# Making the expert layer's normalised tokens and gate scores inside the self-attention loop

## The reference

```python
x = x + _L0_attn_ref(_layernorm(x), L0_attn_W_qkv)     # 16 heads of 32, sequences of 64 tokens
x = x + _L0_ffn_ref(_layernorm(x), L0_ffn_w_gate, L0_ffn_c_fc, L0_ffn_c_proj)

# in _L0_ffn_ref, xf = the normalised tokens, 1024 x 512, w_gate 512 x 8
scores = jax.nn.softmax(xf @ w_gate, axis=-1)
weights, idx = jax.lax.top_k(scores, 2)
# every token goes to its two experts (silu(a) * g, then c_proj); the outputs are weighted and added
```

## Time and the profile before

| what | value |
|---|---|
| median of 3 runs | 2301.62 us (2297.68 to 2303.34) |
| the profiled execution | 2300.68 us, its span 2298.8 us |
| mean granted TensorE clock | 0.934 of full speed |
| TensorE busy, whole span | 2048.7 us (89%) |
| self-attention, first q transpose of tile 0 to that of tile 7 | 178.44 to 311.36 us |
| self-attention, tile 7 until its last product is read | 311.36 to 330.83 us |
| from there to the first routing instruction (L774) | 330.83 to 366.00 us |
| routing, owners and slots | 366.00 to 378.46 us |
| the four weight arrays of L710 | issued 334.40 to 335.82 us, the last landed 18.8 us after its issue |
| scatter, until TensorE's first expert instruction | 378.46 to 406.42 us |

### The profile page before, as it was taken

How to read it: one execution, slowest core, us unless ns; L and a number is a source line. 1 busy time by engine, 2 the same in 40 slices (tenths; PEclk the granted TensorE clock), 3 DMA queues, 4 the chain that set the end, 5 groups by cost and what they waited for, 6 DMA issues and landing times. The chain is left out here.

```text
span 2298.8 us, 29289 instructions
## 1 busy us (share of the span) xinstructions
PE 2048.7 (89%) x9908; PEld 1410.4 (61%) x9908; DVE 1119.8 (49%) x2292; ACT 902.9 (39%) x1668; POOL 122.3 (5%) x137
## 2 busy tenths in 40 slices
PE   7978973899999958999999999999969999867998
PEld 4647762555555547787878777777746666523443
DVE  4655652001101136354453536364448888739992
ACT  5743320111111134444444435354436666525550
POOL 0000003000000011000000000000000000002320
PEclk9989975999999989999999999999988999668999
DMA  7310014787777522010100000012040000010000
GB/s 264 123 51 1 0 65 192 282 315 310 284 314 315 219 69 92 15 46 33 40 32 27 32 27 32 27 46 87 1 162 1 1 1 1 1 78 0 1 14 23
DMA packets 32725, 208.18 MB, mean 91 GB/s; under 512 B 4243, under 2 KB 4244, under 8 KB 25110
## 3 DMA queue, kind: packets, MB, share of 16 engines
q1 hardware_dynamic: 30102, 199.02, 23.0%
q0 software_dynamic: 2560, 8.39, 1.1%
HBM read 186.95 MB, written 20.45 MB: 90 GB/s over the span
## 5 line engine op out<-in xcount | busy, mean ns | idle before, releaser
L108 PE MATMUL PS<-cT,qs 128*128 128x512 f32 x1152 | 295.2, 402 | 9.0 <-ACT pb L1242 7.0
L108 PE MATMUL PS<-pT,cN 128*128 128x512 f32 x1152 | 270.1, 393 | 1.7 <-DVE pT L1337 1.7
L108 PEld LDWEIGHTS PS<-cT,qs 128*128 128x128 f32 x1152 | 209.2, 189 | 59.5 <-issue 15.0
L900 PE MATMUL PS<-W,xgT 128*128 128x384 f32 x736 | 242.8, 489 | 1.4 <-ACT xgT L923 1.4
L108 PEld LDWEIGHTS PS<-pT,cN 128*128 128x128 f32 x1152 | 214.0, 188 | 45.2 <-DVE pT L1337 1.9
L900 PEld LDWEIGHTS PS<-W,xgT 128*128 128x128 f32 x736 | 140.7, 191 | 104.0 <-issue 11.4
L108 PE MATMUL PS<-ws,xT 128*128 128x512 f32 x672 | 183.3, 429 | 6.4 <-DVE ws L571 4.9
L108 PEld LDWEIGHTS PS<-ws,xT 128*128 128x128 f32 x672 | 133.8, 201 | 52.8 <-issue 21.9
L1332 DVE TENSOR_REDUCE nmax<-PS 128x1 f32<-128x512 f32 x128 | 87.7, 685 | 157.0 <-PE PS L108 156.4
L951 DVE TENSOR_TENSOR hid<-gated,PS 128x384 f32<-128x384 f32 x46 | 23.4, 551 | 277.6 <-PE PS L876 235.6
L884 PE MATMUL PS<-W,hT 128*128 128x512 f32 x276 | 124.5, 601 | 10.4 <-ACT hT L917 10.4
(11 more groups left out here) (226 smaller groups left out, 3198.7 us busy)
## 6 DMA issues: line engine op xcount, KB each, us to landing
W<-in_fc SPq DMA_DIRECT2D x23, 3072.0 KB, 12.5
W<-in_proj SPq DMA_DIRECT2D x23, 1536.0 KB, 6.5
cT<-in_ctxT SPq DMA_DIRECT2D x16, 768.0 KB, 5.3
ct_in<-in_ctxT SPq DMA_DIRECT2D x16, 768.0 KB
cn_in<-in_ctxN SPq DMA_DIRECT2D x16, 768.0 KB
W<-in_w SPq DMA_DIRECT2D x2, 4096.0 KB, 12.9
routed_x<-zero SPq DMA_DIRECT2D x23, 256.0 KB, 5.4
xg<-routed_x SPq DMA_DIRECT2D x23, 256.0 KB, 5.7
```

Of the source, the lines that this page charges most:

```text
L108: mm = nc.tensor.matmul(out, lhs(m, s), rhs(n, s), start=(opens and (s, m, n) == terms[0]), stop=((s, m, n) == terms[-1]))
L900: mm = nc.tensor.matmul(ps[c][:, 0:HFE], xgT[:, k, :], fc[u][:, k, c * HFE:(c + 1) * HFE], start=(k == 0), stop=(k == DK - 1))
```

## The change

The normalisation, the GpSimd copy, the transposes and the gate products of the expert layer are issued inside the self-attention's pass. After `x` of tile i is final, VectorE makes its statistics and, behind the copy of v, the normalised tile `gxn`; GpSimd makes the power and copies the tile to `xn`. TensorE transposes tile i-1 behind the projections (`gate_turn`, bank 7), and multiplies it by the gate weights between the first and the second group of probability transposes (`gate_scores`, in a free piece of bank 6); ScalarE copies the transposed tile (`gate_xT`) and the 8 scores per token (`gate_out`) to `logit`. Tile 0 is written out ahead of the loop, since it has no predecessor; tile 7's transposes and products follow at the end. `gate` is loaded at the start of the self-attention. The expert layer's loop over the tiles goes, and its first reduction reads the scores from SBUF. The diff, cut:

```diff
@@ -445,18 +445,43 @@
+        xn, logit = e.xn, e.logit
+        gate, gxT = sbuf("gate3", [P, DK, NE]), sbuf("xT3", [P, DK, P])
+        gxn = sbuf("xn3", [P, D])
+        gst, gmv, gve, grs = sbuf("st3", [P, 6]), sbuf("mv3", [P, 2]), sbuf("ve3", [P, 1]), sbuf("rs3", [P, 1])
+        s_gate, g_var, g_rstd, g_norm = sem("s_gate3"), sem("var3"), sem("rstd3"), sem("norm3")
+        g_turned, g_xT, g_mm, g_sb = sem("turned3"), sem("xT3_sb"), sem("g_mm3"), sem("g_sb3")
+        g_kept, g_seen = sem("kept3"), sem("seen3")
...
+            @block.sync
+            def _(sp):
+                sp.dma_start(gate[:, :, :], a["gate"]).then_inc(s_gate, 16)
...
+                def gate_rstd(i):
+                    pool.wait_ge(g_var, BASE + i + 1)
+                    nc.gpsimd.tensor_tensor(grs[:, :], gve[:, :], cn[:, CN_MHALF:CN_MHALF + 1],
+                                            ALU.pow).then_inc(g_rstd, 1)
+
+                def gate_keep(i):
+                    pool.wait_ge(g_norm, BASE + i + 1)
+                    nc.gpsimd.tensor_copy(xn[:, bass.ds(i, 1), :].rearrange("p o d -> p (o d)"),
+                                          gxn[:, :]).then_inc(g_kept, 1)
...
                     ln.pool(pool, i + 2)
+                    gate_rstd(i)
+                    gate_keep(i)
+                gate_rstd(NT - 1)
+                gate_keep(NT - 1)
...
+                def gate_turn(i):
+
+                    pe.wait_ge(g_norm, BASE + i + 1)
+                    for kk in range(DK):
+                        tr = nc.tensor.transpose(ps[7][:, kk * P:(kk + 1) * P],
+                                                 gxn[:, kk * P:(kk + 1) * P], ident)
+                    tr.then_inc(g_turned, 1)
+
+                def gate_scores(i):
+
+                    pe.wait_ge(g_xT, BASE + i + 1)
+                    for kk in range(DK):
+                        mm = nc.tensor.matmul(ps[6][:, DK * S:DK * S + NE], gxT[:, kk, :], gate[:, kk, :],
+                                              start=(kk == 0), stop=(kk == DK - 1))
+                    mm.then_inc(g_mm, 1)
+
+                pe.wait_ge(s_gate, BASE + 16)
                 ln.tensor(pe, 0)
                 project(0)
 
-                def tile(i, last):
+                def tile(i, first, last):
...
                         project(i + 1)
+                    if not first:
+                        gate_turn(i - 1)
                     pe.wait_ge(e_sb, BASE + 2 * i + 2)
                     for g in TURN:
+                        if not first and g == TURN[1]:
+                            gate_scores(i - 1)
+                        if not first and g == TURN[3]:
+                            pe.wait_ge(g_sb, BASE + i)
...
-                with pe.Fori(0, NT - 1) as i:
-                    tile(i, False)
-                tile(NT - 1, True)
+                tile(0, True, False)
+                with pe.Fori(0, NT - 2) as i:
+                    tile(i + 1, False, False)
+                tile(NT - 1, False, True)
+                pe.wait_ge(o_read, BASE + NT)
+                gate_turn(NT - 1)
+                gate_scores(NT - 1)
...
+                def gate_xT(i):
+                    act.wait_ge(g_turned, BASE + i + 1)
+                    nc.scalar.activation(gxT[:, :, :].rearrange("p k t -> p (k t)"), ps[7],
+                                         ACT.Copy).then_inc(g_xT, 1)
+
+                def gate_out(i):
+                    act.wait_ge(g_mm, BASE + i + 1)
+                    nc.scalar.activation(logit[:, bass.ds(i, 1), :].rearrange("p o e -> p (o e)"),
+                                         ps[6][:, DK * S:DK * S + NE], ACT.Copy).then_inc(g_sb, 1)
...
                     if not last:
                         take(i + 1)
+                    if not first:
+                        gate_xT(i - 1)
                     for g in range(2):
                         act.wait_ge(pt_mm, BASE + 4 * i + TURN.index(g) + 1)
                         act.wait_ge(o_mm, BASE + i)
                         nc.scalar.activation(pT[:, g * DK:(g + 1) * DK, :].rearrange("p m t -> p (m t)"),
                                              ps[3 + g], ACT.Copy).then_inc(pt_act, 1)
-
-                with act.Fori(0, NT - 1) as i:
-                    tile(i, False)
-                tile(NT - 1, True)
+                        if g == 0 and not first:
+                            gate_out(i - 1)
...
+                gate_xT(NT - 1)
+                gate_out(NT - 1)
...
-                    nc.vector.tensor_tensor(x[:, i, :], x[:, i, :], o[:, :], ALU.add)
+                    ch.link(nc.vector.tensor_tensor(x[:, i, :], x[:, i, :], o[:, :], ALU.add))
+                    row = bass.ds(i, 1)
+                    ve.sem_inc(g_seen)
+                    ch.link(nc.vector.bn_stats(gst[:, :], x[:, row, :].rearrange("p o d -> p (o d)")))
+                    ve.sem_inc(g_seen)
+                    ch.link(nc.vector.bn_aggr(gmv[:, :], gst[:, :]))
+                    nc.vector.tensor_scalar(gve[:, :], gmv[:, 1:2], LN_EPS, None, ALU.add).then_inc(g_var, 1)
                     if not last:
                         take_v(i + 1)
+                    ve.wait_ge(g_rstd, BASE + i + 1)
+                    ve.wait_ge(g_kept, BASE + i)
+                    ve.wait_ge(g_turned, BASE + i)
+                    nc.vector.tensor_scalar(gxn[:, :],
+                                            x[:, row, :].rearrange("p o d -> p (o d)"), gmv[:, 0:1], grs[:, 0:1],
+                                            ALU.subtract, ALU.mult).then_inc(g_norm, 1)
...
-            xT = rbuf("xT3", [P, DK, P])
-            gate = rbuf("gate3", [P, DK, NE])
-            ln = Norm(nc, e, "3", rbuf, ps[7], xT)
             TE = [P, NT, NE]
+            scores = e.logit
...
-                    ln.pool(pool, 0)
-                    with pool.Fori(0, NT) as i:
-                        pool.wait_ge(ln.norm, BASE + i + 1)
-                        nc.gpsimd.tensor_copy(xn[:, i, :], ln.xn[:, :]).then_inc(kept, 1)
-                        ln.pool(pool, i + 1)
-
-                    pool.wait_ge(kept, BASE + NT)
...
-                    ln.tensor(pe, 0)
-                    pe.wait_ge(s_gate, BASE + 16)
-                    with pe.Fori(0, NT) as i:
-                        pe.wait_ge(ln.xT_ready, BASE + i + 1)
-                        for k in range(DK):
-                            mm = nc.tensor.matmul(ps[0][:, bass.ds(i * NE, NE)], xT[:, k, :], gate[:, k, :],
-                                                  start=(k == 0), stop=(k == DK - 1))
-                        mm.then_inc(g_mm, 1)
-                        ln.tensor(pe, i + 1)
...
-                    ln.vector_stats(ch, 0)
-                    ln.vector_norm(ve, 0)
-                    with ve.Fori(0, NT) as i:
-                        ch.turn(i, 2)
-                        ln.vector_stats(ch, i + 1)
-                        ve.wait_ge(kept, BASE + i + 1)
-                        ln.vector_norm(ve, i + 1)
-                    ch.base, ch.n = 2 + 2 * NT, 0
-
-                    ve.wait_ge(g_mm, BASE + NT)
-                    lg = ps[0][:, 0:NT * NE].rearrange("p (t e) -> p t e", t=NT)
-                    ch.link(nc.vector.tensor_reduce(r8[:, :], lg, AX.X, ALU.max))
-                    nc.vector.tensor_tensor(logit[:, :, :], lg, wide(r8[:, :]), ALU.subtract).then_inc(s_max, 1)
+                    ch.link(nc.vector.tensor_reduce(r8[:, :], scores[:, :, :], AX.X, ALU.max))
+                    nc.vector.tensor_tensor(logit[:, :, :], scores[:, :, :], wide(r8[:, :]), ALU.subtract).then_inc(s_max, 1)
...
+        with nc.sbuf_tensor("xnall", [P, NT, D], F32) as env.xn, nc.sbuf_tensor("logits", [P, NT, NE], F32) as env.logit:
+            self_attention_layer(nc, a, env)
+            with nc.sbuf_tensor("W1", [P, 2 * (DK * 2 * FE + FE // P * D)], F32) as env.W1:
+                expert_layer(nc, a, env)
+        reset_sems()
```

More of the change, by code:

```diff
@@ L557, in tile @@
                                              ps[3 + g], ACT.Copy).then_inc(pt_act, 1)
-                with act.Fori(0, NT - 1) as i:
-                    tile(i, False)
-                tile(NT - 1, True)
+                        if g == 0 and not first:
+                            gate_out(i - 1)
+                tile(0, True, False)
+                with act.Fori(0, NT - 2) as i:
+                    tile(i + 1, False, False)
+                tile(NT - 1, False, True)
+                gate_xT(NT - 1)
+                gate_out(NT - 1)
             @block.vector
@@ L625, in tile @@
                     ve.sem_inc(o_read, 1)
-                    nc.vector.tensor_tensor(x[:, i, :], x[:, i, :], o[:, :], ALU.add)
+                    ch.link(nc.vector.tensor_tensor(x[:, i, :], x[:, i, :], o[:, :], ALU.add))
[5 more added lines that the diff above has]
+                    nc.vector.tensor_scalar(gve[:, :], gmv[:, 1:2], LN_EPS, None, ALU.add).then_inc(g_var, 1)
                     if not last:
                         take_v(i + 1)
```

(23 more changed lines are left out.)

## The result

The changed kernel takes 2309.68 us (median of 6 runs, 2308.98 to 2310.66) against 2302.43 us for the kernel before (6 runs, 2297.68 to 2303.34): ratio 1.0033, 95% interval 1.0021 to 1.0046. The prediction was 2314.0 us, range 2304 to 2322, slower with a chance of 0.70. It is slower, as forecast, but by less than the 12.4 us that had been summed up: by 7.3 us in the medians, and by 9.1 us in the two profiled executions, whose spans are 2298.8 and 2307.9 us. The 0.3% from which the prediction spoke of a change lies inside the interval, so the direction is measured and "over 0.3%" is not.

What follows compares the result with a forecast made beforehand. TensorE's closed chain per pass, with kT holding the scores, was taken to bound the self-attention. 34.1 us added there, 25.2 removed and 3.5 for the scatter gave +12.4 us, forecast 2314.0 us, range 2304 to 2322.

Steps and rivals of the forecast that it cites:

- Removed: Last self-attention output to first routing instruction: only a single tile's chain stays of the stretch, 25.2 us less.
- VectorE's insertion: Between x and kT in seven passes: kT and the scores start 2.0 us later each, 14.0 us in all.
- TensorE's insertion: Passes of tiles 1 to 6: transposes and gate products delay the second probability group 1.97 us each, 11.8 us.
- The clock: Self-attention passes: longer idle before the scores drops TensorE's clock every pass; projections 4.8, scores 2.7, pT stands -0.9, sum 6.6 us.
- Tile 7: Last self-attention tile: gate products on its path at half clock cost 1.7 us; whole stretch forecast at +4.1.
- The transfers: Routing to first expert instruction: weight arrays still in flight delay the scatter by 3.5 us, between 0 to 1.4 and 5.7.
- 1 (alternation stays): Self-attention passes: clock keeps falling only in every other pass, so +4.9 us, 2306.5; chance 0.15.
- 2 (kT does not hold the scores): Self-attention passes: VectorE's insertion does not reach the scores, the 14.0 us vanish, 2300.0 or 2292.5; chance 0.07.
- 4 (the transfers cost nothing): After the routing starts: weight arrays' transfers add no delay, +8.9 us, 2310.5; inside the forecast, no separate chance.
- Rival 3: Self-attention passes: clock falls earlier and stays low through the narrow work, 30 us more, 2344; chance 0.05.

Runs made afterwards that it cites:

- the run with both edits: The changed kernel with VectorE's statistics and normalisation moved into its wait for the exponentials and the four cross-attention weight arrays loaded early; 2286.72 us, ratio 0.9935.
- the run with eight: The changed kernel plus eight additional 128x512 products with unused results in TensorE's idle time before the scores of tiles 1 to 7; 2296.76 us, ratio 0.9967.

## Why the prediction was right, and by how much its terms were off

**Removed.** 25.2 forecast, 25.64 measured. The tail's steps came within 0.3 us of what was worked out; ScalarE's small copy took 0.18 us, and with its waits the first routing instruction stood 9.53 us behind the last output instead of 10.0.

**VectorE's insertion.** 2.0 us a pass forecast, 3.18 - 1.21 = 1.97 measured, and the run with it moved gave back more than its 14 us. The step held: what counts is not that VectorE has idle time in a pass but where.

**TensorE's insertion.** 1.97 forecast, 1.77 measured; the step mis-sized is the start of the gate products, 1.28 us behind that of the transposes (216.01 to 217.29) instead of 1.49. I had put 0.86 us from the modelled end of the transposes to the products, from a row at half clock; here it is 0.68. The two groups of transposes fill 0.86 us of the 1.28, so by starts TensorE stands for 0.42 us instead of 0.6; the profile lists 0.25 of it as idle. Six times 0.2 are 1.2 us.

**The clock.** 4.8 us forecast for the projections in the passes of tiles 1 to 6, 60.65 - 55.56 = 5.1 measured; the scores 1.28 us in five of the six passes, and no stand on pT any more. With the alternation of the kernel before as its rival, the forecast took the case that came, and the run with only VectorE and GpSimd in the passes shows that the longer wait alone gives this price. But it is only in part how it came: the forecast let the clock fall in the wait, and in the passes of tiles 3 to 6 it fell ahead of the wait, in the transposes of q and k. The fall there costs nothing of its own, since the scores wait for kT: they start 8.88 us behind the products with v, whether the transposes between ran at full clock (219.55 to 228.43) or at half (242.68 to 251.56). That the price came out right all the same is in this part luck.

The Trainium skill ("TensorE: Matmul & The Clock Gate", section "HAM oscillation — how this bites in real kernels") describes a loop in which the wait of each turn makes the next turn's dense work start at half clock. The traces of the changed kernel agree in that every pass pays: its six projections take 9.34 to 10.39 us instead of 8.46. They do not in the detail: in the pass of tile 2 the scores still ran at full clock (0.91 us), and the clock fell only as the projections began. And the kernel before, with a wait of 1.57 us in each turn, paid in every second one.

**Tile 7.** 4.1 forecast, 1.24 measured; this is the largest miss. kT's delay came, and the gate products held up the second group by 1.57 us (353.67 to 355.24), but the clock rose inside the products with v, which took 4.17 us instead of 6.88:

```profile
356.00:358.00 2.00, 2.00 (x12) 2.00 (x10) 0.69 (x1) 0.60 (x1) 0.00 (x0) 0.50 0.00 0
358.00:360.00 2.00, 2.00 (x17) 2.00 (x15) 0.69 (x1) 0.00 (x0) 0.00 (x0) 0.77 0.00 0
360.00:362.00 2.00, 2.00 (x18) 1.89 (x17) 0.00 (x0) 0.00 (x0) 0.00 (x0) 1.00 0.00 0
```

Without that rise tile 7 would have come at 1.24 + 2.71 = 3.95 us, near the forecast, which had no term for it. The other runs have a pattern: where tile 7's scores ran at half clock (1.27 or 1.28 us; the changed kernel, the run with only VectorE and GpSimd in the passes, the one with early loads) these products took 3.98 to 4.18 us, and where the scores took 0.90 to 1.03 us (the kernel before and the other six) they took 6.87 or 6.88. Why stays open.

**The transfers.** 3.5 forecast, 4.56 measured for the scatter, of which the run with early loads took back 4.4; between the two bounds (0 to 1.4 and 5.7) it was nearer the worse one, as taken. Against it stands a gain that was in no step: the routing itself is 1.14 us shorter. Before, ScalarE's exponential stood behind its copy for a ninth, unused tile of the removed loop (VectorE waited 1.45 us for it, now 0.32).

**The start.** Tile 0's first q transpose came 1.39 us later, which no step had: 0.65 before TensorE's first transpose (162.89 instead of 162.24), and 0.76 in the first projections, 11.11 us instead of 10.35, in which the clock came up later. Among the kernels of the experiments, alike up to that point but for a few instructions, the first transpose came between 162.1 and 163.8 and these projections took 9.8 to 11.4 us, so this part varies and is not shown to be the change's.

Of the rivals, 1 (alternation stays) is refuted by the projections, 2 (kT does not hold the scores) by the run with VectorE's work moved, 4 (the transfers cost nothing) by the run with early loads. Rival 3 (the clock stays down through the narrow work) came in a small part, below.

The sum is nearer than its terms: the passes, tile 7, the removal and the routing came out 1.4, 2.9, 0.4 and 1.1 us better than forecast, the start and the scatter 1.4 and 1.1 us worse.

## What to carry to other kernels

The removed loop gave its time back in full, but its work is free only where it goes into a stretch in which its engine waits and nothing behind it is waited for: the same four VectorE instructions cost 2 us a pass in front of kT and nothing visible in the wait for the exponentials, and that move alone turned 0.3% slower into 0.6% faster. Idle time on TensorE was paid twice here, once as itself (2 us a pass) and once as half clock in the dense work that followed (up to 1.9 us in a projection). A loop that goes may also have covered a transfer behind it: look at what was loading in its shadow.

## What the runs showed of the hardware that was not expected

The clock fell in the middle of busy but narrow work. In the changed kernel, from tile 3's pass on, it fell in the transposes of q and k. The first time was at some 246.3 us; TensorE had been at narrow work since 239.13 with one stand of 0.25 us, and the wait in front of the scores was still to come. It stayed at half until some 4 us into the projections (3.7 to 4.1):

```profile
244.00:246.00 2.00, 2.00 (x20) 2.00 (x19) 0.00 (x0) 0.00 (x0) 0.00 (x0) 1.00 0.00 0
246.00:248.00 2.00, 2.00 (x13) 2.00 (x13) 1.36 (x2) 0.60 (x1) 0.00 (x0) 0.57 0.00 0
```

In the kernel before and in the run with only VectorE and GpSimd in the passes, which have none of the added work on TensorE there, the transposes of q and k stayed at 2.4 GHz in every pass. All kernels with the added work have such falls, in the run with VectorE's work moved in five of six passes, although the wait was short there. So they go with the added narrow work; that it is the cause is not shown, for in the run with both edits one fell in the pass of tile 1, ahead of which no added work stands.

And additional dense products with unused results in a wait made a kernel 12.9 us faster. Behind them, in the run with eight, every projection in the passes of tiles 1 to 6 began at 2.4 GHz.
